# Layer 1 of a two-layer transformer on one core: its step order woven from a table of delays, and one of VectorE's subtractions given to GpSimd

## The reference, cut to what matters

```python
h = layernorm(x) * (1 + ca) + sa
Q, K, V = split(h @ w_qkv); Q, K = rope(Q), rope(K)          # 16 heads of 16
attn = softmax(where(causal, Q @ K.T / 4, -1e9)) @ V
x = x + ga * (attn @ w_proj + b_proj)
h = layernorm(x) * (1 + cb) + sb
h = silu(h @ w1.T * s1) * (h @ w2.T * s2)                    # 256 -> 1024, ternary weights
h = gelu(h @ h1.T * s_h1)                                    # 1024 -> 1024
h = gelu(h @ h2.T * s_h2)                                    # 1024 -> 1024
x = x + gb * (h @ w3.T * s3)                                 # 1024 -> 256
```

## Time and profile before

| | us |
|---|---|
| median of 3 runs | 2969.58 (2963.26 to 2972.77) |
| profiled execution, its own time | 2954.33 |
| its span | 2952.6 |
| one pass of the loop over b (A to D), 2114.0 to 2308.6 us | 194.6 |
| window D of that pass | 97.7 |

### The profile page before, as it was taken

How to read it: one execution, slowest core, us unless ns; L and a number is a source line. 1 busy time by engine, 2 the same in 40 slices (tenths; PEclk the granted TensorE clock), 3 DMA queues, 4 the chain that set the end, 5 groups by cost and what they waited for, 6 DMA issues and landing times.

```text
span 2952.6 us, 42635 instructions
## 1 busy us (share of the span) xinstructions
PE 2413.2 (82%) x17541; PEld 1880.7 (64%) x17541; DVE 1347.4 (46%) x2536; ACT 1060.0 (36%) x1670; POOL 300.4 (10%) x503
## 2 busy tenths in 40 slices
PE   5888888888888888665669788898898888988988
PEld 3667666666666666453247666676576666766787
DVE  4445454545444544333245444444453444544444
ACT  1536262636353636221324233133332332333321
POOL 1101020202111111000101001011010000100100
PEclk9999999999999999856779989899898998998999
DMA  1000000000000000172000000000000000000000
GB/s 58 9 8 8 8 9 8 9 8 9 8 9 8 9 8 1 45 254 80 1 1 5 1 12 5 1 12 5 12 5 1 12 4 1 16 1 4 5 5 9
DMA packets 56483, 49.29 MB, mean 17 GB/s; under 512 B 12896, under 2 KB 52064, under 8 KB 56288
## 3 DMA queue, kind: packets, MB, share of 16 engines
q1 hardware_dynamic: 52064, 42.33, 4.7%
q10 hardware_dynamic: 4224, 4.19, 0.4%
HBM read 26.33 MB, written 8.39 MB: 12 GB/s over the span
## 4 chain that ended last, share of the span: by engine, by line
PE 39%; DVE 8%; ACT 6%; issue 2%; DMA 2%; POOL 1%; SPq 1%; DVEq 0%; ACTq 0%; POOLq 0%
PE b_ps L1793 19%; PE b_ps L1720 4%; PE b_ps L1684 4%; PE b_ps L1732 3%; DVE b_nat L1436 3%; ACT b_work L1569 2%; PE b_ps L1824 2%; PE b_ps L1716 2%; ACT b_work L1621 1%; PE b_ps L1748 1%; DVE b_work L1497 1%; DMA b_work<-in_L_ffn_h_w 1%; DVE b_work L1496 1%; DVE b_acts L1508 1%; PE b_ps L1704 1%
## 5 line engine op out<-in xcount | busy, mean ns | idle before, releaser
L1621 ACT ACTIVATE b_work<-b_ps,b_s 128x256 f32<-128x256 f32 x256 | 107.5, 471 | 539.6 <-PE b_ps L1793 539.6
L1793 PEld LDWEIGHTS b_ps<-b_acts,b_h2T 128*128 128x128 f32 x2048 | 255.6, 196 | 22.0 <-issue 18.0
L1793 PE MATMUL b_ps<-b_acts,b_h2T 128*128 128x256 f32 x2048 | 267.2, 290 | 2.2 <-DVE b_acts L1508 2.2
L1793 PE MATMUL b_ps<-b_acts,b_h1T 128*128 128x256 f32 x2048 | 261.8, 287 | 2.2 <-DVE b_acts L1500 1.4
L1793 PEld LDWEIGHTS b_ps<-b_acts,b_h1T 128*128 128x128 f32 x2048 | 251.9, 193 | 12.9 <-issue 7.6
L1436 DVE TENSOR_REDUCE b_nat<-b_ps 128x4 f32<-128x2048 f32 (+3 forms) x128 | 187.7, 1487 | 131.7 <-PE b_ps L1720 131.7
L713 ACT ACTIVATE a_work<-a_ring 128x512 f32<-128x512 f32 x320 | 177.4, 602 | 120.2 <-PE a_acc L913 63.1
L1507 DVE CAST b_acts<-b_work 128x512 fp32r<-128x512 f32 x128 | 54.7, 427 | 361.6 <-ACT b_work L1621 361.6
L1569 ACT ACTIVATE b_work<-b_ps 128x2048 f32<-128x2048 f32 (+1 forms) x96 | 153.2, 1596 | 85.6 <-PE b_ps L1732 85.5
L1331 POOL TENSOR_SCALAR_AFFINE_SELECT b_work<-b_work 128x512 f32<-128x512 f32 x128 | 83.3, 662 | 861.3 <-ACT b_work L1569 861.3
L820 PE MATMUL a_ring<-a_ident,a_naturals 128*128 128x128 f32 x1024 | 131.5, 278 | 42.0 <-DVE a_naturals L562 41.1
(11 more groups left out here) (232 smaller groups left out, 4354.4 us busy)
## 6 DMA issues: line engine op xcount, KB each, us to landing
b_work<-in_L_ffn_h_w SPq DMA_DIRECT2D x16, 512.0 KB, 6.1
a_xin<-in_L_attn_x SPq DMA_DIRECT2D x8, 512.0 KB, 3.9
x_mid<-a_xn ACTq DMA_DIRECT2D x8, 512.0 KB, 3.5
b_h1T<-b_work SPq DMA_DIRECT2D x8, 512.0 KB, 5.2
b_h2T<-b_work SPq DMA_DIRECT2D x8, 512.0 KB, 4.9
b_x<-x_mid SPq DMA_DIRECT2D x8, 512.0 KB, 4.0
out<-b_x SPq DMA_DIRECT2D x16, 256.0 KB, 2.1
b_work<-in_L_ffn_w_w SPq DMA_DIRECT2D x6, 512.0 KB, 5.5
```

Source lines behind the costliest of these rows:

```text
L1621: ins = nc.scalar.activation(full[nth % 2][:, j * HALF:(j + 1) * HALF], here[:, j * HALF:(j + 1) * HALF], ACT.Gelu, scale=s12[:, 2 + (name ...
L1793: ins = nc.tensor.matmul(dst, view(w[:, k, m * P:(m + 1) * P]), view(src[:, k, i]), start=(k == 0 and i == 0), stop=(k == nk - 1 and i == 1))
```

## The change

1. `merge` is replaced by `weave`. It takes chains of steps and walks a clock. `needs(step)` names, for each step, the steps that it follows and a delay after each. Of the chains whose next step is due, the one named first gives its step; if none is due, the one that is due soonest. In D there are now three chains, in this order of preference: the rest of n, the start of m, the hidden layers of b.
2. The steps `h1`, `h2` (32 matmuls) and `last` are cut in two halves of 16 each in the list, so that another step can come between. ACT and DVE still act once for each pair, at the second half.
3. The first layernorm of m is cut in two steps: `stats` (statistics, and the power on POOL) at the start of C, `norm` (the four normalising instructions) at the start of D, where its wait on the value products is for one fewer.
4. The low part of a gated unit (subtraction of 128 x 256, both inputs in SBUF) moves from DVE to POOL. DVE signals the high part (`a_high`), POOL then signals `a_ready`, for which the tanh two units later and the first `h1` product wait.
5. Some costs in `COST` are changed.

```diff
+def needs(step):
+    name, b = step[:2]
+    if name == "hT":
+        return [(("norm", b), 2.0)]
+    if name == "proj":
+        t = step[2]
+        return [(("hT", b), 2.0)] + ([(("proj", b, t - 2), 2.6)] if t >= 2 else [])
+    if name in ("tq", "tk"):
+        return [(("proj", b, step[2]), 3.2 + 0.4 * (name == "tk"))]
...
+    if name == "turn":
+        return [(("heads", b, 2 * step[2] + 1), 1.5)]
+    if name == "out":
+        return [(("turn", b, 0), 1.3), (("turn", b, 1), 1.3)]
+    if name == "xT":
+        return [(("out", b, 1), 6.5)]
...
+def weave(clock, done, chains):
...
+    while any(chains):
+        heads_of_chains = [chain for chain in chains if chain]
+        now = [chain for chain in heads_of_chains if ready(chain[0]) <= clock]
+        chain = now[0] if now else min(heads_of_chains, key=lambda c: ready(c[0]))
+        step = chain.pop(0)
+        clock = max(clock, ready(step)) + COST[step[0]]
+        done[step] = clock
+        out.append(step)
...
     for b in range(-2, B):
         n, m = b + 1, b + 2
...
+        window(weighted(n, 0), [("split", b, 0)] + [("last", b - 1, 1, t) for t in range(2)] + gated_units(b, 0))
+        window([("heads", n, 1)] + maxima(n, 2) + [("ga", n), ("gb", b)] + maxima(n, 3), hidden(b, 0))
+        window([("stats", m)] + weighted(n, 2), [("split", b, 1)] + [("last", b, 0, t) for t in range(2)] + gated_units(b, 1))
+        window([("norm", m), ("heads", n, 3), ("turn", n, 0), ("turn", n, 1), ("out", n, 0), ("out", n, 1), ("xT", n)],
+               [("hT", m)] + [("proj", m, 0), ("proj", m, 1), ("tq", m, 0), ("tk", m, 0), ("proj", m, 2), ("tq", m, 1), ("tk", m, 1), ("proj", m, 3),
+                              ("tq", m, 2), ("tk", m, 2), ("tq", m, 3), ("tk", m, 3)] + maxima(m, 0) + maxima(m, 1), hidden(b, 1))
...
+                elif name == "up":
+                    half, i = step[2:]
+                    pool.wait_ge(a_high, (b * 2 + half) * NHID + i + 1)
+                    nc.gpsimd.tensor_tensor(act_a[:, i, 1], th[i % 2], act_a[:, i, 0].bitcast(F32), ALU.subtract).then_inc(a_ready, 1)
...
                     dve.sem_inc(free, 1)
-                    link(nc.vector.tensor_copy(act_a[:, i, 0], z))
-                    nc.vector.tensor_tensor(act_a[:, i, 1], z, act_a[:, i, 0].bitcast(F32), ALU.subtract).then_inc(a_ready, 1)
+                    nc.vector.tensor_copy(act_a[:, i, 0], z).then_inc(a_high, 1)
```

143 lines of the change are left out of this document (84 added, 59 removed).

## The result

The changed kernel takes 2745.24 us, the median of 4 runs (2741.65 to 2752.52). The kernel before took 2966.42 us (4 runs, 2956.14 to 2972.77). The ratio is 0.9261, with a 95% interval of 0.9226 to 0.9295. The direction was as predicted, and so were the waits in D, but not what the clock does behind them.

The account below looks back on a forecast made before the run. PE bounds the kernel by work, and its waits, mostly in D, also slow its clock. Terms -159 - 15 + 12 - 3.5 - 4 = -169.5 gave 2784.8 us in the profile, 2800 for the median, range 2755 to 2885.

Parts of the forecast that it names:

- 0, give or take 3: The two passes before b = 0, with no hidden steps to fill with: no change, give or take 3 us.
- The step that failed: Window D: a longest wait of 2.5 us leaves one slow-clock stretch of some 10 us, about 4 us lost.
- From the profile to the median: The forecast profile time of 2784.8 us was raised to a median of 2800, the runs' median being 15.3 above the profiled execution.
- The work in D: PE's work in window D at full clock: 61.5 us, 12.6 of its 74.1 busy us given back.
- The waits in D: PE's waits left in window D by the new order: 5.7 us in sum, the longest 2.5 before `tq` 1.
- A and C: Windows A and C: A gains 2.5 us in each of six passes (-15), C has hardly anything to give.
- B: Window B: new waits at `gb` (1.0) and one `max` (0.7) cost 1.7 us each, +12 in seven passes.
- POOL: Subtraction moved to POOL: 0.7 us each, 0 to 1 us per window, -3.5 us in the last pass.
- The rival that has it slow: POOL's queue in A and C slows the kernel: 2985 us if each subtraction with its wait takes 4.2; chance 0.03.
- b = 6: The pass with D without m: the wait for `turn` and the slow stretch behind it shrink, -4 us.
- half the gain: D's waits twice as large (11.4 us) from queues and shared banks, clock still slow: median 2900 us; chance 0.27.
- Nearly all of it: No slow stretch, `tq` 1 in time, B without cost, D at 65 us: 2750 us; chance 0.12.

Follow-up runs that it names:

- experiment 1: The changed kernel with the low-part subtraction back on DVE: 2764.59 us, ratio 0.932 to the kernel before.
- experiment 8: The changed kernel with one unneeded DVE instruction ahead of the second rotation, lengthening the wait before `tq` 1: 2758.80 us, ratio 0.931 to the kernel before.
- experiment 7: The changed kernel with two unneeded DVE instructions ahead of the second rotation, lengthening the wait before `tq` 1: 2760.95 us, ratio 0.932 to the kernel before.
- experiment 9: The changed kernel with delays added to the order's table for the four places where queues and banks bite: 2745.97 us, ratio 0.928 to the kernel before.
- experiment 10: The changed kernel with a mask put ahead of the subtraction directly before it in POOL's queue: 2747.86 us, ratio 0.928 to the kernel before.
- experiment 12: The changed kernel with masks first on POOL and the delay table retuned (queue delays, `turn` spacing, shorter delays after `max`): 2697.69 us, ratio 0.912 to the kernel before.

## Why the prediction was right, and where it was not

Per stretch, in the profiled executions, from the rows above and those of before (b = 0 took 185.5 us before, b = 1 to 5 together 972.8):

| | predicted | measured |
|---|---|---|
| up to b = 0 | 0 | -4.4 |
| one pass: A | -2.5 | -3.7 |
| one pass: B | +1.7 | +1.3 |
| one pass: C | 0 | -1.1 |
| one pass: D | -26.5 | -31.0 |
| passes b = 0 to 5 | -164 | -194.9 (-24.8, then 5 x -34.0) |
| b = 6 | -2.3 | -10.3 |
| last pass (113.3 to 110.2) | -3.5 | -3.1 |
| sum | -169.5 | -212.7 |

A to D are those of the two middle passes shown, and above. The pass b = 0 gained less than the other five, since it was shorter before and has the one slow stretch in D. Of the 4.4 us up to b = 0 none is the change's: the first layernorm of layer 1 begins 6.2 us earlier in this execution (1344.0 instead of 1350.2), ahead of everything that was edited, and 1.8 are lost from there to b = 0, where "0, give or take 3" was said.

- **The step that failed** is the one that reads "The longest is 2.5, about as long as the 2.40 between `max` steps now, so I leave one slow stretch of some 10 us in D". The wait was there (2.24) and the slow stretch was not, in five of the six D, and in the sixth it was 6.8 us long and not 10. That is 4 of the 4.5 us by which this D was missed, and some 20 of the 43 in all. The premise, that a wait of that length brings a slow stretch, does not hold in the trace of before for the wait that it names: there the clock fell ahead of the 2.40, behind waits of 1.71, 0.77 and 0.77 (before 2265.0, 2273.2 and 2275.1). The stretches up to that fall, from it to the end of PE's work, and the wait itself:

```profile
2271.40:2275.80 4.40, 2.87 (x26) 2.28 (x28) 1.12 (x2) 2.99 (x6) 0.00 (x0) 1.00 0.02 4
2275.80:2277.67 1.87, 1.87 (x8) 0.30 (x8) 0.00 (x0) 0.00 (x0) 0.00 (x0) 0.50 0.00 0
2277.67:2280.07 2.40, 0.01 (x1) 0.00 (x0) 2.29 (x1) 0.00 (x0) 0.00 (x0) 0.50 0.00 0
```

The two falls after it do lie behind a wait of 2.31 and in one of 2.84. Experiments 1 and 8 show that a wait of 2.24 or 2.70 can have a slow stretch behind it or not, in one and the same kernel, and experiments 7 and 8 that it comes more often with more of it. What decides in a single pass stays open.
- **From the profile to the median.** 15.3 us were added for the median, since before it lay so far above the profiled execution. For the changed kernel it lies 3.6 above. Of the 55 us between 2800 and 2745, 43 are the profile's and 12 are this step.
- **The work in D** was said to be 61.5 us at full clock, from the mean clock and the busy time. It is 61.9: that way of reading held. (In the trace of before, 25.7 us of PE's work in D lie at 0.50, half of which is 12.8, where 12.6 was said.)
- **The waits in D** were said to be 5.7 and are 4.8: `turn` 1.0 (0.81), `tq` 1 2.5 (2.24), `proj` 3 1.3 (1.15), `max` 0.7 (0.41), `tq` 0 0.2 (0.21). Each was worked out from what stands on DVE and in the shared bank, not from the table's delays.
- **A and C** were missed by 1.2 and 1.1 us. In both PE's idle time went from 1.7 to 1.0, and its work is 3.1 us shorter in A (the clock, 0.92 before) and 0.5 in C. The waits for exponentials and masks that stood there are hidden by the new order, but for the one behind a subtraction (1.02). "0 and not more than 1 us per window" was just about right for that place (1.02), and wrong in that nothing was set on the other side.
- **B** was said to lose 1.7 and lost 1.3. Its waits are `ga` 0.68, `gb` 0.72 and 0.35 at one `max`, against the 1.19 of the earlier trace rows: 0.6 more, where I had put 1.7. The other 0.7 is PE's work, 42.06 us against 41.31. A part of it is where the stretches are cut (that of before begins inside `heads`); for the rest I have no cause.
- **POOL** was right: 0.7 said, 0.73 measured (below), 388.8 us busy in all against "near 390". The rival that has it slow is refuted: the move saves 13 to 19 us. But its gain was set to 3.5 us (the last pass alone), and experiment 1 shows several times that, most of it through the clock. The last pass itself gained 3.1. A gated unit there waits 0.37 at every second unit instead of 0.55 at each, and the first `h1` 0.83 for POOL instead of 0.69 for DVE.
- **b = 6** was said to gain 4 in D and gained 10.3 in the pass. Work fell from 131.2 to 125.9, so half is again the clock (0.96 to 1.00).
- **The rival "half the gain"** was given 0.27 for the queues that the table does not know. They do bite, at the four places named, but that rival needed them twice as large. "Nearly all of it" (2750: no slow stretch, `tq` 1 in time, B without cost) is the closest in time, and only the first of its three conditions came true, in five D of six.

In the sum of the middle pass this is the clock once more: of the 34.5 us gained, 15.0 are the clock, where the prediction had 12.6 for D less 4, and 2.5 in A.

## What to carry to other kernels

Price the idle time of TensorE twice: once as it stands, once as the clock that falls behind it, and give the second a chance of its own, since one and the same wait can have it behind it in one pass and not in the next. Where an order is made from a table of delays, look for the queue that a step really stands in (another engine's instructions ahead of its producer, a bank that must be emptied first): the table of this kernel was right to within 0.5 us in B and D everywhere but at four places (`ga` and `gb` taken as one). Mending these alone gave nothing, since the work to fill with ran out at the end. It paid when the filling was spread as well and the masks went first (experiments 9, 10 and 12); which share of the 54 us the spreading has was not measured by itself. And to relieve an engine off the critical path may still be worth it, if it shortens what stands before a wait.
